# A graph aggregation on one core: weights moved from the one-hot to the gathered rows, and three matrix products made one

## The reference, cut to what matters

```python
xn = _layernorm(x, axis=-1)
msgs = edge_vals[:, None] * x[edge_src]                        # x is xn here
agg = segment_sum(msgs, edge_dst, num_segments=N)              # 6250 x 256
deg = maximum(segment_sum(ones, dst, num_segments=6250), 1.0)  # edges per node
...
deg = segment_sum(ew, dst, num_segments=n_nodes) + 1.0         # second layer: weights per node
```

## Time and profile before

| what | value |
|---|---|
| time, median of 3 runs | 4422.07 us (4420.8 to 4436.18) |
| span of the profiled execution | 3913.9 us, mean granted TensorE clock 0.897 |
| own time of the profiled execution | not listed; the span is 508.2 us below the median |
| TensorE matmul busy | 2817.2 us (72% of the span) |
| VectorE busy | 1759.8 us (45%) |
| ScalarE busy | 768.9 us (20%) |
| GpSimd busy | 2555.5 us (65%) |

### The profile page before, as it was taken

The page is one execution under the profiler, slowest core; times in us unless marked ns, Lnnn a source line. Parts: engine busy times, 40 slices in busy tenths (PEclk is TensorE's granted clock), DMA queues, the critical chain, the costliest instruction groups (busy, mean ns, idle before and its releaser), DMA issues. The chain is left out here.

```text
span 3913.9 us, 41587 instructions
## 1 busy us (share of the span) xinstructions
PE 2817.2 (72%) x12730; PEld 2139.6 (55%) x12730; DVE 1759.8 (45%) x4424; ACT 768.9 (20%) x1634; POOL 2555.5 (65%) x2689
## 2 busy tenths in 40 slices
PE   3577877777768647667777777665677777777778
PEld 2466656656544535556555555544466555556557
DVE  6433335555524842443333333332355555555533
ACT  1111101111103313321111111110122222222210
POOL 3677777777760342557777777775777777777701
PEclk9999988888879879889989999887889999999969
DMA  4344434444433457754444444433344444444405
GB/s 139 116 117 120 124 107 139 130 138 131 129 96 94 143 164 202 213 179 133 138 117 125 124 125 125 114 111 97 109 123 122 124 124 123 123 121 125 125 21 197
DMA packets 279533, 501.68 MB, mean 128 GB/s; under 512 B 59771, under 2 KB 179969, under 8 KB 279162
## 3 DMA queue, kind: packets, MB, share of 16 engines
q0 software_dynamic: 126240, 345.85, 30.9%
q1 hardware_dynamic: 135916, 139.10, 11.5%
q10 hardware_dynamic: 17136, 13.84, 1.1%
HBM read 419.12 MB, written 79.18 MB: 127 GB/s over the span
## 5 line engine op out<-in xcount | busy, mean ns | idle before, releaser
L1476 PE MATMUL bank<-g,m 128*128 128x256 f32 (+1 forms) x4704 | 1466.0, 436 | 806.4 <-DMA g<-d_t,src_i 537.4
L1399 POOL DMA_INDIRECT g<-d_t,src_i x1568 | 1505.2, 960 | 511.4 <-issue 511.4
L1476 PEld LDWEIGHTS bank<-g,m 128*128 128x128 f32 x4704 | 879.6, 211 | 1102.3 <-issue 400.1
L1399 POOL DMA_INDIRECT g<-d_xn,src_i x784 | 802.3, 1023 | 244.3 <-issue 242.5
L1424 DVE TENSOR_SCALAR m<-iota,rel_f,ew_f 128x128 f32<-128x128 f32 x1568 | 421.6, 365 | 255.9 <-PE bank L1476 250.4
L1440 DVE TENSOR_TENSOR accT<-bank,accT 128x256 f32 x294 | 122.8, 418 | 593.1 <-PE bank L1464 592.9
L1405 ACT ACTIVATE s<-bank 128x256 f32<-128x256 f32 (+1 forms) x294 | 111.4, 379 | 1076.0 <-PE bank L1478 554.7
L1427 DVE TENSOR_TENSOR eq<-iota,rel_f 128x1024 bf16<-128x1024 f32 x98 | 119.9, 1224 | 138.3 <-PE bank L1478 138.3
L1478 PE MATMUL bank<-ones_b,eq 128*128 128x1 bf16 x784 | 136.9, 175 | 0.0
L1340 PE MATMUL bank<-wg,side_lg 128*128 128x256 f32 (+1 forms) x392 | 132.1, 428 | 2.9 <-DVE side_lg L1332 2.9
L219 POOL TENSOR_TENSOR rsd<-ved,mhalf 128x2 f32<-128x2 f32 (+1 forms) x25 | 19.0, 760 | 175.6 <-DVE ved L213 175.4
(11 more groups left out here) (387 smaller groups left out, 4273.3 us busy)
## 6 DMA issues: line engine op xcount, KB each, us to landing
g<-d_t,src_i POOLq DMA_INDIRECT x1568, 2.8
side_xn<-d_xn SPq DMA_DIRECT2D x96, 256.0 KB, 3.1
g<-d_xn,src_i POOLq DMA_INDIRECT x784, 2.8
d_swT<-wkv SPq DMA_DIRECT2D x48, 256.0 KB, 3.0
swT<-d_swT SPq DMA_DIRECT2D x24, 512.0 KB, 3.8
xt<-d_xs POOLq DMA_DIRECT2D x80, 128.0 KB, 3.0
d_ys<-y ACTq DMA_DIRECT2D x80, 128.0 KB, 2.6
x<-in_x SPq DMA_DIRECT2D x24, 256.0 KB, 2.7
```

The source lines that it names most:

```text
L1399: pool.indirect_dma_start(g[n % RING][:, u, 0:D], None, table, bass.IndirectOffsetOnAxis(ap=k.src_i[:, t:t + 1], axis=0)).then_inc(gathere ...
L1476: ins = pe.matmul(b[:, 0:GW], m[o][:, u, :], g[r][:, u, :], start=(u == 0), stop=(u == GT - 1 and not count))
```

## The change

Only the aggregation with `count` changes.

- VectorE builds one plain 32-bit one-hot per tile with a compare (8 small operations per group in place of two large ones); `eq` in bf16 is gone.
- The gathered buffers have 258 columns in place of 257. Column 256 gets the edge's weight, column 257 holds ones and is set once.
- ScalarE gets `weigh(n, h)` for each half of a group, at slots 2, 5, 10 and 13 of the round, ahead of the side steps of the same slot: it waits for the half's four gathers, copies the four weights into column 256, and multiplies the 256 gathered columns of each tile in place by the edge's weight, one activation per tile with a scale read per partition.
- TensorE waits for `scaled` from ScalarE in place of `gathered`, and does one product of 258 columns per tile in place of one of 257 and one of a single column.
- The setup no longer sets `ones_b`.

```diff
-    GW = D + 1 if count else D
-    SW = GW + 1 if count else D
+    SW = D + 2 if count else D
...
-        g = [st.sb(f"g{r}", [P, GT, GW]) for r in range(RING)]
+        g = [st.sb(f"g{r}", [P, GT, SW]) for r in range(RING)]
...
-        eq = [st.sb(f"eq{r}", [P, GT, P], BF16) for r in range(ONEHOTS)] if count else []
...
+            def weigh(n, h):
+                rows_of, at = g[n % RING], n * GT + 4 * h
+                wait(act, gathered[n % RING][h], 64 * (n // RING + 1))
+                act.activation(rows_of[:, 4 * h:4 * h + 4, D:D + 1], k.ew_f[:, at:at + 4].rearrange("p (u a) -> p u a", a=1), ACT.Copy)
+                for u in range(4):
+                    ins = act.activation(rows_of[:, 4 * h + u, 0:D], rows_of[:, 4 * h + u, 0:D], ACT.Copy, scale=k.ew_f[:, at + u:at + u + 1])
+                ins.then_inc(scaled, 1)
             for i in range(ROUNDS):
                 for slot in range(2 * GT):
                     if slot == 1 and 0 < i <= NB:
                         copy(2 * i - 1)
                     if slot == 9 and i < NB:
                         copy(2 * i)
+                    if count and slot in (2, 5, 10, 13) and 2 * i + slot // GT < NG:
+                        weigh(2 * i + slot // GT, slot % GT // 4)
                     at_step(side.act, slot, i)
...
+                for u in range(GT):
+                    t = n * GT + u
+                    if count:
+                        ins = dve.tensor_scalar(m[r][:, u, :], k.iota[:], k.rel_f[:, t:t + 1], None, ALU.is_equal)
+                    else:
                         ins = dve.tensor_scalar(m[r][:, u, :], k.iota[:], k.rel_f[:, t:t + 1], k.ew_f[:, t:t + 1], ALU.is_equal, ALU.mult)
-                dve.tensor_tensor(eq[r][:], k.iota[:].rearrange("p (a n) -> p a n", a=1).to_broadcast([P, GT, P]),
-                                  k.rel_f[:, e].rearrange("p (u a) -> p u a", a=1).to_broadcast([P, GT, P]), ALU.is_equal).then_inc(eq_done, 1)
-                wait(dve, eq_done, n + 1)
-                dve.tensor_tensor(m[r][:], eq[r][:], k.ew_f[:, e].rearrange("p (u a) -> p u a", a=1).to_broadcast([P, GT, P]), ALU.mult).then_inc(m_done, 1)
+                ins.then_inc(m_done, 1)
...
-                    ins = dve.memset(g[r][:, :, D:D + 1], 1.0)
+                    ins = dve.memset(g[r][:, :, D + 1:SW], 1.0)
...
-                if u % 4 == 0:
+                if u % 4 == 0 and count:
+                    wait(pe, scaled, 2 * n + u // 4 + 1)
+                elif u % 4 == 0:
                     wait(pe, gathered[r][u // 4], 64 * (n // RING + 1))
-                ins = pe.matmul(b[:, 0:GW], m[o][:, u, :], g[r][:, u, :], start=(u == 0), stop=(u == GT - 1 and not count))
-                if count:
-                    ins = pe.matmul(b[:, GW:SW], eq[o][:, u, :], k.ones_b[:, 0:1], start=False, stop=(u == GT - 1))
+                ins = pe.matmul(b[:, 0:SW], m[o][:, u, :], g[r][:, u, :], start=(u == 0), stop=(u == GT - 1))
```

More of the change, by code:

```diff
@@ L343, in _ @@
                 then(dve.tensor_copy(edst[0:NG, :], epad_i[0:NG, 1, :]))
-                then(dve.memset(k.ones_b[:], 1.0))
                 then(dve.tensor_reduce(okc[0:NG, 0:1], edst[0:NG, :], AX.X, ALU.min))
@@ L391, in go @@
                     return k.bank[(kk - 1) % 2]
-                pe.wait_ge(step, 12)
+                pe.wait_ge(step, 11)
                 for x in (esrc, edst, rel, eew):
@@ L1375, in stage_aggregate @@
         gathered = [[st.pool_dma(f"gathered{r}_{h}") for h in range(2)] for r in range(RING)]
-        eq_done, m_done, multiplied, copied, window_turned, acc_added, ones_set = (
-            st.sem(n) for n in ("eq_done", "m_done", "multiplied", "copied", "window_turned", "acc_added", "ones_set"))
+        m_done, multiplied, copied, window_turned, acc_added, ones_set, scaled = (
+            st.sem(n) for n in ("m_done", "multiplied", "copied", "window_turned", "acc_added", "ones_set", "scaled"))
         blank, cleared, row_loaded, dup_done, idx_done, weighted, row_done, scattered, at_loaded, at_turned = (
@@ L1418, in prepare @@
                 r = n % ONEHOTS
-                e = slice(n * GT, (n + 1) * GT)
                 wait(dve, multiplied, n - ONEHOTS + 1)
-                if not count:
-                    for u in range(GT):
-                        t = n * GT + u
-                        ins = dve.tensor_scalar(m[r][:, u, :], k.iota[:], k.rel_f[:, t:t + 1], k.ew_f[:, t:t + 1], ALU.is_equal, ALU.mult)
-                    ins.then_inc(m_done, 1)
-                    return
-                dve.tensor_tensor(eq[r][:], k.iota[:].rearrange("p (a n) -> p a n", a=1).to_broadcast([P, GT, P]),
-                                  k.rel_f[:, e].rearrange("p (u a) -> p u a", a=1).to_broadcast([P, GT, P]), ALU.is_equal).then_inc(eq_done, 1)
-                wait(dve, eq_done, n + 1)
-                dve.tensor_tensor(m[r][:], eq[r][:], k.ew_f[:, e].rearrange("p (u a) -> p u a", a=1).to_broadcast([P, GT, P]), ALU.mult).then_inc(m_done, 1)
+                for u in range(GT):
[3 more added lines that the diff above has]
+                    else:
+                        ins = dve.tensor_scalar(m[r][:, u, :], k.iota[:], k.rel_f[:, t:t + 1], k.ew_f[:, t:t + 1], ALU.is_equal, ALU.mult)
+                ins.then_inc(m_done, 1)
             def finish(n):
@@ L2652, in build @@
         k.ew_f = sb("ew_f", [P, NET])
-        k.ones_b = sb("ones_b", [P, 1], BF16)
         k.src_i = sb("src_i", [P, NET], I32)
```

## The result

The changed kernel takes 4452.61 us (median of 19 runs, 4434.79 to 4476.93) and the kernel before 4422.07 on the same chip (19 runs): a ratio of 1.0073, 95% interval 1.0052 to 1.0093. It is slower by 30 us where 42 us less were forecast. (Per tile, two products became one; the title speaks of three.)

A forecast was written before the change was run, and what follows sets the result against it. GpSimd's gathers were taken to bound the first aggregation: 49 us saved by shorter gathers, less 2 at the stage's end and 5 for late TensorE, gave 42 us, so 4422.1 to 4380 us; range 4368 to 4500.

The forecast's parts named there:

- GpSimd sets the pace, TensorE follows: First aggregation: GpSimd's 784 gathers bound the stage at 1041 us, waiting only 1.8 us for TensorE.
- 508.2 us between span and median: Whole kernel: profiled span 3913.9 us, 508.2 below the median; the 42 us gain was taken off both alike.
- The gathers go from 1.023 to 0.960: First aggregation: mean gather falls from 1.023 to 0.960 us without the big VectorE operations, saving 49 us.
- TensorE's chain: First aggregation: 628 us of products, 265 of waits for weighing and 97 of low clock make 990 us.
- The weighing is hidden under GpSimd's floor: First aggregation: TensorE's 990 us with weighing waits still fits under the gathers' 992 us, so GpSimd keeps the pace.
- Rival 1: Wait before each group's first tile: TensorE becomes the bound as its clock falls; chance 0.32 slower, 0.12 no difference.

The follow-up runs named there:

- e1: The kernel before, unchanged, run for a second profile: 4367.75 us in its single run.
- e9: The kernel before, first aggregation uncoupled: GpSimd gathers without waiting for TensorE, TensorE multiplies old rows without waiting for gathers; 1.1175 of the kernel before, 4949.84 us.
- e6: The kernel before without the gathers of groups 4 to 97 of the first aggregation: 0.8948 of the kernel before.
- e3: The kernel before with two small VectorE operations per tile in place of two large ones per group, no weighing by ScalarE: 1.0018 of the kernel before.
- e4: The changed kernel with the weighing left out, TensorE waiting for the gathers and column 256 holding ones: 0.9957 of the kernel before.
- e12: The changed kernel without ScalarE's weighing: weights back in the one-hot, column 256 ones, column 257 the inverse weight, one product per tile; 0.9923 of the kernel before.
- e7: The changed kernel without the gathers of groups 4 to 97 of the first aggregation: 0.9571 of the kernel before.
- e18: e12 with a ring of six half groups of gathered rows in place of eight: 0.9899 of the kernel before, 4377.93 us.
- e17: e12 with a ring of nine half groups of gathered rows in place of eight: 0.9957 of the kernel before.

## Why the prediction was wrong

By its own steps:

- *GpSimd sets the pace, TensorE follows.* This is the step that failed. It was read from the earlier trace rows, where GpSimd waits 1.8 us for TensorE. In e1, whose time is that of the timed runs, it waits 109 us, and the two engines aren't independent: their joint stage (1150 us) is longer than either chain alone (1047 by the sum, 1072 beside an uncoupled TensorE in e9; 715 in e6). With it fails the rule behind the sum, that the stage is the longer of two chains. In the nine runs that keep the coupling and have neither the weighing behind the copy nor stops of their own, the stage is 1134 to 1158 us, whatever the gathers' mean (0.971 to 1.031), the bytes, the number of products or the ring.
- *508.2 us between span and median.* I took the gain off both alike, as if the difference lay around the span. It lay in it: of the 452 us between that span and e1's, 416 are idle time of GpSimd before the gathers of the three aggregations. The row that warned was the span itself.
- *The gathers go from 1.023 to 0.960.* Right in kind: 1.031 to 0.973, 46 us of the 49. By the rule of the Trainium skill weighed there (page "SBUF — State Buffer", section "Who interferes with whom") the new compares would have blocked the gathers as the old operations did. They hardly do: the 144 gathers of after that start during one take 0.987 us on average, the other 640 0.970. In e1 the 99 that start during the old compare take 1.499. But the 46 us bought nothing: GpSimd reaches the full ring sooner and stops for longer (e3, e4, e12).
- *TensorE's chain.* Without gathers it is as predicted: 628 + 97 us of products are 716 of busy time, 265 us of waits 282.5, and the chain of 990 is 994 (e7). An activation costs 0.504 us for the 0.50 estimated (after).
- *The weighing is hidden under GpSimd's floor.* Not hidden. TensorE is held up beside the gathers as it is, and with its waits for ScalarE on top GpSimd waits for it longer: 195 us in all for 141 without the weighing (e4). So the weighing costs 48 us of stage (1182 against 1134), the rest of the change gives 16 (1134 against 1150), and 32 are lost.
- *Rival 1* had the place (the wait before a group's first tile), the sign and the sight (gathers short, GpSimd waiting for products), but not the cause. Its clock fell to 0.84:

```profile
121.60:1310.00 1188.40, 759.06 (x3029) 599.95 (x3029) 415.05 (x1184) 470.55 (x1309) 762.80 (x784) 0.84 0.37 109
```

  e1 has 0.82 in the same stage without the change, and the changed chain alone, with all its waits, has 0.91 and 994 us. From e7 to after TensorE's busy time grows by 43 us (716 to 759) and the stage by 188. So the clock can account for some 43 us; the rest comes with the gathers beside the chain.

Why the execution profiled first escaped the late signals stays open. All eighteen runs have GpSimd's stops in their second aggregation, 44 to 48 of them, and so has the profile of after; the earlier trace rows have none, so sums of before can't be read from that profile. The two kinds of execution also differ in what was recorded. Of all the profiles only that one tells when the gathers landed (before, then e1):

```profile
g<-d_xn,src_i POOLq DMA_INDIRECT x784, 2.8
g<-d_xn,src_i POOLq DMA_INDIRECT x784
```

Its trace has 53838 semaphore events of DMAs, that of e1 21617 for the same program. Whether the recording has a part in holding TensorE up was not tried; every run of the experiments is listed with a span and a clock, so it was recorded.

The best version found is not the change but e12 or e18, with weights back in the one-hot and one product: 0.992 and 0.990 of before (an edge of weight zero isn't counted there). By the intervals of e12, e17 and e18 the three can hardly be told apart.

## What to carry to other kernels

Before a profile's "never waits" carries a sum, lay its span beside the measured time: here 11% were missing, and the missing part was waiting. Two engines that only look independent are best tested by uncoupling them, once with each left out and once side by side. And work that is put between two engines should stand ahead of the hand-over its engine waits for: behind the copy the weighing cost 48 us of stage, ahead of it 6.

## What the runs showed of the hardware

While GpSimd issues indirect gathers one after the other, a gather per 1.25 us, TensorE can fall to one instruction per 1.40 us and stand still for 12 to 55 us at a time, although the two share no wait (e9). Its signals then reach the other engines late, by some 9 us in the timeline of after and by 43 in that of e9. The Trainium skill's page "SBUF — State Buffer", section "Who interferes with whom", says that TensorE and ScalarE never wait on anyone. It says so of SBUF's ports, and no run shows whether a port is involved; but e9 and e6 have 427 matrix products in 1072 us beside the gathers and 3854 in 715 us without, so as a rule for TensorE beside indirect gathers the measurement decides against it, in these recorded executions.

The same section's statement that a VectorE operation with two inputs from SBUF contends with a GpSimd instruction that reads SBUF agrees with the earlier trace rows for the compare: in e1 the 80 gathers that start in it with over 0.2 us of it left end a median 0.82 us after it. It doesn't hold for the multiplication of line 1430, which also has two inputs from SBUF, and here the prediction had read the earlier trace rows too widely. A gather that starts in the compare's last 0.2 us runs on beside that multiplication at its usual length, 0.951 us on average (19 of them in e1, at most 0.986):

```profile
290.24 1.23 DVE L1427 TENSOR_TENSOR eq<-iota,rel_f 128x1024 bf16<-128x1024 f32 x1 [2.69 <-issue]
291.30 0.99 POOL L1399 DMA_INDIRECT g<-d_xn,src_i  x1 [0.30 <-issue]
291.50 1.22 DVE L1430 TENSOR_TENSOR m<-eq,ew_f 128x1024 f32<-128x1024 bf16 x1
```
